# Two tiles of 25, in place of one, built from feature columns on the chip; the copies addressed by bytes

## The reference, cut to what matters

```python
# x: 12500 nodes x 128; src, dst: 400000 edges, sorted by dst; ea: 400000 x 32
h  = relu(layernorm(x))
m  = relu(concat(h[src], h[dst], ea) @ w1 + b1) @ w2 + b2
agg = segment_sum(m, dst, num_segments=12500)
gi, gh = agg @ w_ih + b_ih, h @ w_hh + b_hh
r  = sigmoid(gi_r + gh_r);  z = sigmoid(gi_z + gh_z);  n = tanh(gi_n + r * gh_n)
out = x + (1 - z) * n + z * h
```

## Time and profile before

| | |
|---|---|
| median of three runs | 3851.58 us |
| the profiled execution | 3857.86 us, its span 3856.0 us |
| POOL busy | 2861.7 us (74%), 3000 gathers |
| PE busy | 2920.9 us (76%) |
| DVE busy | 2076.1 us (54%) |
| ACT busy | 1921.0 us (50%) |
| granted TensorE clock | 0.733 of full speed |

### The profile page before, as it was taken

One profiled execution on the slowest core, in us unless ns is written; L12 is line 12 of the kernel. 1 busy time (PEld: TensorE's weight loads), 2 busy tenths in 40 slices (PEclk: granted clock), 3 DMA queues, 4 the chain that ended last, 5 costly groups with the idle time before them and its releaser, 6 DMA issues.

```text
span 3856.0 us, 94141 instructions
## 1 busy us (share of the span) xinstructions
PE 2920.9 (76%) x16157; PEld 2660.2 (69%) x16157; DVE 2076.1 (54%) x8517; ACT 1921.0 (50%) x13700; POOL 2861.7 (74%) x3039
## 2 busy tenths in 40 slices
PE   4677877777777778778777777777787787787777
PEld 4666767667667767667767776677676776677676
DVE  5555555555555555555555555555555555555554
ACT  5544555445554545445554455445554455545553
POOL 4677777777777777777777777777777777777775
PEclk8677677777777776776776677767767767767766
DMA  6444444444444444444444444444444444444443
GB/s 172 118 112 112 111 111 112 111 114 112 111 111 112 111 111 111 111 112 112 111 112 112 112 111 111 111 112 111 111 112 111 114 112 111 112 112 111 111 111 80
DMA packets 439213, 433.42 MB, mean 112 GB/s; under 512 B 180040, under 2 KB 331047, under 8 KB 439057
## 3 DMA queue, kind: packets, MB, share of 16 engines
q0 software_dynamic: 96000, 196.80, 23.5%
q1 hardware_dynamic: 314864, 223.36, 19.7%
q10 hardware_dynamic: 28318, 12.94, 1.2%
HBM read 419.89 MB, written 12.82 MB: 112 GB/s over the span
## 4 chain that ended last, share of the span: by engine, by line
POOL 51%; issue 23%; PE 14%; DMA 3%; ACT 3%; ACTq 2%; DVE 1%; POOLq 1%; DVEq 0%; SPq 0%
POOL rows L488 51%; PE ps L1194 6%; DMA rows<-p_rows,idx 3%; ACT picked L654 2%; ACTq L645 2%; PE ps L1174 2%; PE ps L1209 2%; PE ps L1211 1%; PE ps L1208 1%; DVE rows L934 1%; PE ps L1179 1%; PE ps L1212 1%; POOLq L257 0%; POOLq L285 0%; DVE low L946 0%
## 5 line engine op out<-in xcount | busy, mean ns | idle before, releaser
L488 POOL DMA_INDIRECT rows<-p_rows,idx x3000 | 2831.3, 944 | 938.5 <-issue 897.5
L654 ACT COPY picked<-hT 128x1 f32 x12000 | 1181.4, 187 | 552.9 <-issue 552.9
L1174 PE MATMUL ps<-rhs,lhs 128*128 128x128 f32 x6250 | 1113.4, 342 | 73.5 <-DVE rows L934 68.1
L1194 PE MATMUL ps<-onehot,rows 128*128 128x95 f32 x6250 | 1079.8, 338 | 112.5 <-DVE low L946 112.3
L1194 PEld LDWEIGHTS ps<-onehot,rows 128*128 128x128 f32 x6250 | 1039.0, 255 | 150.8 <-issue 150.8
L934 DVE TENSOR_TENSOR rows<-rows,ps 128x640 f32<-128x640 f32 x625 | 495.6, 793 | 1145.8 <-DMA rows<-p_rows,idx 1138.5
L1174 PEld LDWEIGHTS ps<-rhs,lhs 128*128 128x128 f32 x6250 | 1025.3, 252 | 105.2 <-DVE rows L934 71.5
L660 ACT ACTIVATE rows<-rows 128x640 f32<-128x640 f32 x625 | 447.0, 715 | 1214.0 <-DVE rows L934 1210.6
L902 DVE TENSOR_SCALAR_CACHE_REDUCE lhs<-dst_row,node_at 95x640 f32<-95x640 int32 x625 | 543.2, 869 | 5.3 <-DMA dst_row<-in_dst_rows_dram 5.3
L893 DVE TENSOR_TENSOR onehot<-dst_rel,ps 128x475 f32<-128x475 f32 x625 | 400.9, 642 | 0.0
L925 DVE COPY picked<-hT 128x1 f32 x4000 | 349.9, 146 | 8.0 <-DMA low<-in_src_tiles_dram 7.6
(11 more groups left out here) (101 smaller groups left out, 1372.0 us busy)
## 6 DMA issues: line engine op xcount, KB each, us to landing
dst_row<-in_dst_rows_dram SPq DMA_DIRECT2D x625, 240.0 KB, 3.8
lhs<-in_ea_t_dram SPq DMA_DIRECT2D x625, 80.0 KB
rows<-p_rows,idx POOLq DMA_INDIRECT x3000
idx<-in_src_cols_dram SPq DMA_DIRECT2D x625, 2.5 KB
p_rows<-low SPq DMA_DIRECT2D x14, 448.0 KB, 3.2
x_fin<-in_x_dram ACTq DMA_DIRECT2D x123, 50.0 KB
out_dram<-out_fin ACTq DMA_DIRECT2D x123, 50.0 KB
acc<-in_x_dram SPq DMA_DIRECT2D x13, 448.0 KB, 4.8
```

The lines of the kernel that those rows point to most:

```text
L488: pool.indirect_dma_start(out=rows[:, s, t, :], out_offset=None, in_=p_rows[:, :], in_offset=bass.IndirectOffsetOnAxis(ap=idx[:, s, t:t + ...
L654: last = nc.scalar.copy(picked[:, e:e + 1], hT[:, bass.ds(node, 1)])
L1174: last = nc.tensor.matmul(pre_ps[s % 2][:, t * D:(t + 1) * D], lhs[:, s, t, 0:P], rhs[:, k, :], start=True, stop=gathered)
L1194: done = nc.tensor.matmul(sg[:, 0:W], rows[:, s, t, :], onehot[:, ONEHOT_PLACE[s], t, 0:W], start=(first and t == 0), stop=(last and t == ...
```

## The change

Two tiles of a chunk, tile 4 of group 3 and tile 4 of group 4, are now built from columns of `hT`; 23 are gathered. `picked` holds 256 columns. ScalarE copies 24 in each of the five steps, VectorE 32, 24, 24, 24 and 32. The node numbers are multiplied by 4 and offset by the byte address of `hT` once in setup, written to HBM and read back into ten rows (one for each engine and step); the copies are typed as four bytes, and take their source address from the loaded register. VectorE loads its registers in front of `add_pre`, and makes half of its copies in front of `build_onehot` and half behind it. TensorE waits for a group's second relu only in front of the tile that needs the bank.

```diff
-PICKED = 3
-PICKS_DVE = (8, 8, 8, 8, 0)
-PICKS_ACT = (24, 24, 24, 24, 0)
+PICKED = (3, 4)
+ACT_PICKS = ((0, 24), (56, 24), (104, 24), (152, 24), (200, 24))
+DVE_PICKS = ((24, 32), (80, 24), (128, 24), (176, 24), (224, 32))
+HT_AT = 66688
 def gather_tiles(s):
-    return T - 1 if s == PICKED else T
+    return T - 1 if s in PICKED else T
...
+            sp.dma_start(places.rearrange("c (k p) -> c k p", p=P), picked_tiles).then_inc(src_in, 16)
...
+                sp.wait_ge(places_ready, 1)
+                sp.dma_start(pick_dram, places).then_inc(places_stored, 16)
+                sp.wait_ge(places_stored, 16)
+                for k in range(G):
+                    for row, (first, n) in ((pick_act[k], ACT_PICKS[k]), (pick_dve[k], DVE_PICKS[k])):
+                        sp.dma_start(row.rearrange("o (c e) -> o c e", e=n),
+                                     pick_dram.rearrange("(o c) e -> o c e", o=1)[:, :, first:first + n]).then_inc(pick_in, 16)
...
+            dve.wait_ge(src_in, 16)
+            nc.vector.tensor_scalar(places, places, 4, HT_AT, ALU.mult, ALU.add).then_inc(places_ready, 1)
...
             def load_picks(c, s):
-                if isinstance(c, int) and c == 0:
-                    dve.wait_ge(pick_in, 32)
-                _, nodes = nc.values_load_multi_w_load_instructions(
-                    pick_dve[0:1, bass.ds(c * N_DVE + sum(PICKS_DVE[:s]), PICKS_DVE[s])], (mybir.EngineType.DVE,),
-                    min_val=0, max_val=N - 1, skip_runtime_bounds_check_because=IN_RANGE)
-                return nodes
+                if isinstance(c, int) and c == 0 and s == 0:
+                    dve.wait_ge(pick_in, 32 * G)
+                first, n = DVE_PICKS[s]
+                wait(dve, pre_ready[PICKED[first // P]], c)
+                _, found = nc.values_load_multi_w_load_instructions(
+                    pick_dve[s][0:1, bass.ds(c * n, n)], (mybir.EngineType.DVE,),
+                    min_val=HT_AT, max_val=HT_AT + 4 * (N - 1), skip_runtime_bounds_check_because=IN_RANGE)
+                return found
-            def pick_columns(c, s, nodes):
-                wait(dve, pre_ready[PICKED], c)
-                for e, node in enumerate(nodes, sum(PICKS_DVE[:s])):
-                    last = nc.vector.tensor_copy(picked[:, e:e + 1], hT[:, bass.ds(node, 1)])
-                last.then_inc(picked_dve, 1)
+            def pick_columns(c, s, found, part):
+                first = DVE_PICKS[s][0]
+                for k in part:
+                    e = 4 * (first + k)
+                    last = nc.vector.tensor_copy(picked_bytes[:, e:e + 4], hT_bytes[:, bass.ds(found[k] - HT_AT, 4)])
+                if part[-1] == len(found) - 1:
+                    last.then_inc(picked_dve, 1)
...
                     if s in ENDS:
                         sum_counts(c, ENDS[s])
+                    found = load_picks(c, s)
+                    half = DVE_PICKS[s][1] // 2
                 if s != 1 and old:
                     add_pre(*old)
+                if exists((c, s)):
+                    pick_columns(c, s, found, range(half))
                 if old:
                     build_onehot(*old)
-                if exists((c, s)) and PICKS_DVE[s]:
-                    pick_columns(c, s, load_picks(c, s))
+                if exists((c, s)):
+                    pick_columns(c, s, found, range(half, len(found)))
...
                 for t in range(T):
                     gathered = t < gather_tiles(s)
+                    if t == T - 1 and old and old[1] in PICKED:
+                        pe.wait_ge(message_ready[old[1]], old[0] * 2 + 2)
                     last = nc.tensor.matmul(pre_ps[s % 2][:, t * D:(t + 1) * D], lhs[:, s, t, 0:P],
                                             rhs[:, k, :], start=True, stop=gathered)
                     if not gathered:
-                        pe.wait_ge(picked_dve, (c + 1) * sum(n > 0 for n in PICKS_DVE))
-                        pe.wait_ge(picked_act, (c + 1) * sum(n > 0 for n in PICKS_ACT))
-                        last = nc.tensor.matmul(pre_ps[s % 2][:, t * D:(t + 1) * D], picked[:], w1_keep[:], start=False, stop=True)
+                        slot = PICKED.index(s)
+                        pe.wait_ge(picked_dve, c * G + turns_of(DVE_PICKS, slot))
+                        pe.wait_ge(picked_act, c * G + turns_of(ACT_PICKS, slot))
+                        last = nc.tensor.matmul(pre_ps[s % 2][:, t * D:(t + 1) * D], picked[:, slot * P:(slot + 1) * P], w1_keep[:],
+                                                start=False, stop=True)
```

More of the change, by code:

```diff
@@ L59, with turns_of @@
 PGAP = P + 4
-PICKED = 3
-PICKS_DVE = (8, 8, 8, 8, 0)
-PICKS_ACT = (24, 24, 24, 24, 0)
-N_DVE, N_ACT = sum(PICKS_DVE), sum(PICKS_ACT)
-assert N_DVE + N_ACT == P
-IN_RANGE = "src holds node indices, 0 to N - 1"
+PICKED = (3, 4)
+ACT_PICKS = ((0, 24), (56, 24), (104, 24), (152, 24), (200, 24))
+DVE_PICKS = ((24, 32), (80, 24), (128, 24), (176, 24), (224, 32))
+assert sorted(e for first, n in ACT_PICKS + DVE_PICKS for e in range(first, first + n)) == list(range(len(PICKED) * P))
+def turns_of(picks, slot):
+    return max(k + 1 for k, (first, _) in enumerate(picks) if first < (slot + 1) * P)
+HT_AT = 66688
+IN_RANGE = "src holds node indices, 0 to N - 1, and they are made into places in a row of hT"
 BASE_IN_RANGE = "the window's base is a least node index, and a minimum holds it at BMAX"
@@ L118, in gnn_kernel, with pick_row @@
         at += 2 * NB * D
[L120 to L125, removed]
+        base_i = low[ED:ED + 1, NPAD - CHUNKS * NSETS:NPAD].bitcast(I32)
+        assert at <= NPAD - CHUNKS * NSETS
+        def pick_row(part, at, picks):
+            out = []
+            for _, n in picks:
+                out.append(low[part:part + 1, at:at + CHUNKS * n].bitcast(I32))
+                at += CHUNKS * n
+            assert at <= N
+            return out
+        pick_act = pick_row(ED, 0, ACT_PICKS[:4]) + pick_row(2 * ED, 0, ACT_PICKS[4:])
+        pick_dve = pick_row(2 * ED, CHUNKS * ACT_PICKS[4][1], DVE_PICKS[:2]) + pick_row(3 * ED, 0, DVE_PICKS[2:])
         dst_int = sb("dst_int", [P, G * T], I32)
@@ L642, in load_picks @@
             def load_picks(c, s):
-                if isinstance(c, int) and c == 0:
-                    act.wait_ge(pick_in, 32)
-                _, nodes = nc.values_load_multi_w_load_instructions(
-                    pick_act[0:1, bass.ds(c * N_ACT + sum(PICKS_ACT[:s]), PICKS_ACT[s])], (mybir.EngineType.Activation,),
-                    min_val=0, max_val=N - 1, skip_runtime_bounds_check_because=IN_RANGE)
-                return nodes
-            def pick_columns(c, s, nodes):
[L652 to L655, removed]
+                if isinstance(c, int) and c == 0 and s == 0:
+                    act.wait_ge(pick_in, 32 * G)
+                first, n = ACT_PICKS[s]
+                wait(act, pre_ready[PICKED[first // P]], c)
+                _, found = nc.values_load_multi_w_load_instructions(
+                    pick_act[s][0:1, bass.ds(c * n, n)], (mybir.EngineType.Activation,),
+                    min_val=HT_AT, max_val=HT_AT + 4 * (N - 1), skip_runtime_bounds_check_because=IN_RANGE)
+                return found
+            def pick_columns(c, s, found, part):
+                first = ACT_PICKS[s][0]
+                for k in part:
+                    e = 4 * (first + k)
+                    last = nc.scalar.copy(picked_bytes[:, e:e + 4], hT_bytes[:, bass.ds(found[k] - HT_AT, 4)])
+                if part[-1] == len(found) - 1:
+                    last.then_inc(picked_act, 1)
             def relu_message(c, s):
@@ L699, in step @@
                     relu_message(*old)
-                if exists((c, s)) and PICKS_ACT[s]:
-                    pick_columns(c, s, load_picks(c, s))
+                if exists((c, s)):
+                    pick_columns(c, s, load_picks(c, s), range(ACT_PICKS[s][1]))
                 if s == 0 and ending is not None:
```

37 lines of the change are left out of this document (21 added, 16 removed).

## The result

The changed kernel takes 4087.92 us (median of four runs, 4085.2 to 4088.55), against 3852.61 us for the kernel before in the same comparison (3850.6 to 3860.34): ratio 1.0603, 95% interval 1.0591 to 1.0616. It is slower by 6%. The profiled execution took 4088.32 us, its span is 4086.6 us.

A forecast was written before the change was run, and what follows sets the result against it. VectorE was to replace POOL as the bound: 13.2 + 8.6 copies + 9.0 idle + 0.15 gaps = 30.95 us a chunk, against 29.90; 3857.9 + 131 + 5 = 3994, less 6 for the median, said as 3990 us, range 3730 to 4130.

The forecast's parts named there:

- POOL stops being the bound: One gather fewer leaves POOL 28.65 us a chunk; VectorE binds at 30.95, gathers waiting some 2.3 us for TensorE's sums.
- The loads' length: VectorE's register loads in the five steps: 1.82 us for 24 registers, 2.3 us for 32.
- the factor 1.16: VectorE's single-register load over ScalarE's, 529 / 457 ns, used to scale ScalarE's load of 24 to VectorE.
- What covers them: VectorE's work handed out before a load hides only that much of it; 9.0 us idle a chunk remains.
- A queue twice as deep: If VectorE's queue held twice as many, eight more queued copies would cover steps 0, 1 and 3: 29.5 us a chunk.
- The copies: VectorE makes 136 copies a chunk instead of 32, at 0.063 us each: 8.6 us.
- ScalarE and TensorE: Neither binds: ScalarE needs 23 us of 31 a chunk, TensorE 23.5 plus one matmul of under 0.8.
- The start: Node numbers go to HBM and back before VectorE's first copy: +5 us, once.
- Short loads: Rival: VectorE loads 24 registers in 0.83 to 1.3 us, POOL binds, 3701 us; chance 0.13.
- those in between: Rival: 24 registers load in 1.3 to 1.6 us, VectorE binds under 29.9 us, 3705 to 3840 us; chance 0.15.
- The copies keep 0.118 us: Rival: VectorE's copies stay at 0.118 us each, 7.5 us more a chunk, some 4900 us; chance 0.02.
- The copies stop POOL: Rival: four-element copies hold a port POOL needs for gather descriptors, 37.3 us a chunk, 4780 us; chance 0.03.

The follow-up runs named there:

- The loads in halves: Changed kernel with each long VectorE load and its copies split in two, sum_counts behind the addition; 0.9763 to 0.9823 of the kernel before in four comparisons.
- the late counts: Changed kernel with sum_counts of steps 2 and 4 moved behind the addition of the step before; 5102.9 us, 1.0049 of the kernel before.
- the fixed columns: Changed kernel without VectorE's five long loads, its copies taking fixed columns (part of the picked features wrong); 0.9613 and 0.9748 of the kernel before.
- The copies of one number: Changed kernel without VectorE's long loads, copies from fixed columns, each moving one fp32 number instead of four bytes; one run, 4905.58 us.
- the loads behind the one-hot: Kernel with the loads in halves, but VectorE's loads whole and behind the one-hot, all copies after them; 5012.73 us, 1.0002 of the kernel before.

## Why the prediction was right

The forecast was 3990 us, VectorE bound by its loads. The time is 98 us above it, and inside the forecast's own range.

**POOL stops being the bound: right.** The gathers keep their 944 ns and wait for TensorE's sums. Without their own issue these waits are 3.0 us a chunk and not 2.3, since the chunk is 31.7 us and not 30.95.

**The loads' length: right, the scaling by luck.** Steps 1 and 3 load 24 registers in 1.82 us (1.82 said), step 2 in 1.61, and 32 take 2.17 in step 0 and 2.11 in step 4 (2.3 said); together 9.5 us where 10.1 was said. ScalarE's row was the right neighbour, and going on along VectorE's own line from 1 to 8 registers would have missed by half. But the factor 1.16, from the loads of one register, has no ground: in the changed kernel these take 532 and 286 ns, a factor of 1.86, and the medians of 24 are 1826 and 1500, 1.22. The medians of the earlier trace rows also hide two levels. The load of 8 took 0.60 us in steps 0 and 2 and 0.82 in steps 1 and 3; "620" lies between them. From 8 to 24 registers it is 63 ns a register at either level, more than the 44 of the slowest eight.

**What covers them: right, step by step.** Idle time of the chunk shown, with the forecast in brackets: step 0 1.59 (1.3), step 1 0.63 (0.8), step 2 0.20 + 1.73 (2.2), step 3 1.22 (1.2), step 4 2.20 (2.7), the single load 0.61 (0.8). Together 8.2 against 9.0. The trace takes each idle time apart: the load, plus the time from its end to the next instruction's start, less the time for which VectorE still had work when the load began. The medians over the loop are 2.17 + 0.15 - 0.74 = 1.58 us for step 0, then 1.82 + 0.05 - 1.24 = 0.63, 1.61 + 0.15 - 0.02 = 1.74, 1.82 + 0.12 - 0.72 = 1.22 and 2.11 + 0.12 - 0.02 = 2.21. The middle term is never over 0.15 us, so nothing but the load stands in these gaps, and behind `sum_counts` (steps 2 and 4) it has no cover. One term was wrong: in step 0 no seven copies were queued. The sequencer closes the loop there, and its load begins 0.14 us after `lhs` does, so the 0.4 us of cover were missing. A queue twice as deep, which the prediction weighed, was not what was lacking in steps 1 and 3: only two and one instructions stood in it when the load began. The loads in halves, the late counts and the fixed columns each took away their part of the idle time.

**The copies: mis-sized.** The step was 136 x 0.063 = 8.6 us. VectorE's busy time grew from 13.2 us to 23.3, which leaves 10.1 for them. Queued copies come every 71 ns, 9.7 us for 136; I had taken three more elements at the price of an addition's, 1 ns each, and they cost 10 ns a copy. Of the other 0.4 us the trace explains 0.27: of 15752 copies right behind another, 734 start 80 ns or more after it, and 729 of these 100 to 150 ns into a gather. So a gather's start holds copies back, beside what its end does (below). So two errors partly cancel: 1.5 us more here and 0.7 us less idle time make the +0.75 us a chunk, 94 us, by which the forecast fell short.

**ScalarE and TensorE: off the path, as said.** ScalarE is busy 17.1 us a chunk and idle 3.9 in front of its copies, 21.0 where 23 was said, and TensorE is busy 21.9; all of VectorE's idle time of note is put down to its own issue, none to these two.

**The start:** VectorE's first copy begins at 114.4 us, before at 106.05; +5 was said, +8 it is.

**The rivals.** Short loads, and those in between, fell with the loads' durations. *The copies keep 0.118 us*: no, they start 71 ns apart. *The copies stop POOL*: no in the changed kernel, whose gathers have the same median and reach over 1000 ns 17 times in 2875. The contact is real but it falls mostly on the other side. VectorE's copies last up to 429 ns there, 2351 of 17000 over 250 ns. 98 in 100 of those begin 530 to 705 ns into a gather, nearly every copy that begins there is among them, and they end with the gather, 936 to 959 ns after its start. The copies of one number show none. The Trainium skill (SBUF — State Buffer, "two separate sides") says that a two-port operation of VectorE and an operation of GpSimd share a pair of ports, and that whichever starts first holds it while the other waits; its box names the case in which GpSimd cannot write descriptors. This case's trace fits the rule in the direction that the box does not name: it is VectorE's copies that wait, up to 429 ns. It differs in the extent: copies are held at a gather's start, by 10 to 70 ns, and in its last 0.4 us, but those that begin 150 to 500 ns into it are not and last 157 to 169 ns (98 in 100). Gathers that last longer are there too, in some kernels of the study: 137 of 2875 over 1000 ns with fixed columns, 177 to 191 with the halves, 108 with the late counts, but 7 with the loads behind the one-hot. What makes the difference was not taken apart.

**Open:** that the halves reach POOL's bound, some 3700 us, on a chip like that of the result. The rows say so (VectorE's 23.3 us, 1.6 us in front of the additions and 0.8 for the single loads stay under 28.65), no run does; with the halves' longer gathers POOL's bound itself would be 0.4 us a chunk higher, some 3750 us.

## What to carry to other kernels

An engine's busy share leaves out its sequencer, so before giving an engine more work that is addressed by registers, add up what its sequencer does and ask of each load how much work was handed out ahead of it. Do not put a long load behind a wait on the engine's own result, and cut it so that each piece is no longer than its cover. Moving the whole load to where the most work is in hand took the idle time from the additions, but other waits came in its place, and that kernel was no faster than the one before. The price of a load is to be read from a row with as many registers, not drawn on from a short one, and step by step, since a median can lie between two levels.

## What the runs showed of the hardware

- A load of registers from SBUF on VectorE: 1 register 0.53 us, 8 0.60 or 0.82, 12 0.85 or 1.07, 16 1.10, 24 1.61 or 1.82, 32 2.1 to 2.2. Each place in the loop keeps to one of the two levels; what sets it was not found. From 8 to 24 it is 63 ns a register at either level ((1.61 - 0.60) / 16, (1.82 - 0.82) / 16). ScalarE loads 24 in 1.49 or 1.67.
- Four bytes cost 10 ns more a copy than one fp32 number of the same width. Copies of four bytes are held up beside gathers, those of one number never (at most 157 ns); the small TENSOR_SCALAR of L912 is held too, up to 478 ns.
- The same program took 3852 us on one chip and 4930 to 5120 on four others, with VectorE's instructions as long as before, and gaps of 0.3 to 1.2 us in front of plain ones: on ScalarE in the kernel before, on ScalarE and VectorE in the changed one. What holds them up was not found.
